# Sparse attention in pairs of batches: score rows in thirteen full tiles, values held in TensorE, probabilities divided on GpSimd

## The reference

```python
qkv = x @ qkv_w.T + qkv_b
q, k, v = (qkv[0], qkv[1], qkv[2])
true_scores = einsum('bhnd,bhmd->bhnm', q, k) * scale
pred_scores = einsum('bhnd,bhmd->bhnm', ex_quant(q), ex_quant(k))   # sign and power of two only
_, idx = top_k(pred_scores, 32)
topk_attn = softmax(take_along_axis(true_scores, idx))
attn = zeros.at[idx].set(topk_attn)
out = einsum('bhnm,bhmd->bhnd', attn, v) @ proj_w.T + proj_b
```

## Time and profile before

| | us |
|---|---|
| median of 3 runs | 1248.48 |
| lowest and highest | 1245.09, 1254.43 |
| the profiled execution, its own time | 1248.79 |
| its span in the profile | 1247.0 |
| first `take8` starts | 56.43 |
| last `finish` of the stage starts | 525.47 |

### The profile page before, as it was taken

The page is one execution under the profiler, slowest core; times in us unless marked ns, Lnnn a source line. Parts: engine busy times, 40 slices in busy tenths (PEclk is TensorE's granted clock), DMA queues, the critical chain, the costliest instruction groups (busy, mean ns, idle before and its releaser), DMA issues.

```text
span 1247.0 us, 24432 instructions
## 1 busy us (share of the span) xinstructions
PE 881.7 (71%) x6616; PEld 750.0 (60%) x6616; DVE 753.1 (60%) x4773; ACT 329.2 (26%) x1042; POOL 529.8 (42%) x745
## 2 busy tenths in 40 slices
PE   4788988898989898667400099987778656757830
PEld 4788878888888787444200088987556333633630
DVE  1399999999999999444553444334445344424533
ACT  0234433333433343144200033211111222213410
POOL 3244444444544443245376500043443544454235
PEclk9778888787878655555555599987775676878975
DMA  5123332323233330086021555444785544447833
GB/s 189 33 69 110 141 110 89 109 89 109 90 109 111 113 113 25 19 208 162 7 79 67 169 196 188 149 126 126 256 318 205 182 146 151 140 154 229 272 127 95
DMA packets 81318, 167.70 MB, mean 134 GB/s; under 512 B 12944, under 2 KB 39376, under 8 KB 79536
## 3 DMA queue, kind: packets, MB, share of 16 engines
q1 hardware_dynamic: 55824, 111.18, 27.5%
q10 hardware_dynamic: 14112, 32.12, 7.4%
q0 software_dynamic: 11264, 23.09, 6.3%
HBM read 84.81 MB, written 81.53 MB: 133 GB/s over the span
## 4 chain that ended last, share of the span: by engine, by line
PE 36%; DVE 32%; issue 18%; POOL 5%; DMA 4%; another core or an unknown queue 2%; ACT 2%; DVEq 1%; SPq 0%; POOLq 0%; ACTq 0%
DVE work L1301 13%; DVE top L1295 9%; PE bank L1166 6%; PE bank L1163 5%; PE bank L1212 5%; PE bank L1152 4%; PE bank L1210 3%; POOL early L700 2%; PE bank L1201 2%; PE bank L1099 1%; PE bank L925 1%; PE bank L984 1%; PE bank L1006 1%; POOL slots_g L707 1%
## 5 line engine op out<-in xcount | busy, mean ns | idle before, releaser
L1301 DVE MATCH_REPLACE8 work<-top,work 102x68 f32<-102x68 f32 x1024 | 204.7, 212 | 0.0
L1534 DVE COPY place<-bank 96x256 f32<-96x256 f32 x196 | 74.5, 416 | 149.2 <-PE bank L1152 98.3
L1295 DVE MAX8 top<-work 102x8 f32<-102x68 f32 x1024 | 145.5, 213 | 3.2 <-ACT tru L767 1.9
L1152 PE MATMUL bank<-ident,early 128*96 128x128 f32 x392 | 73.4, 316 | 102.9 <-DMA early<-slots_x 101.2
L886 ACT ACTIVATE m_y<-bank 128x128 f32<-128x128 f32 x196 | 52.5, 278 | 304.2 <-PE bank L1166 207.9
L1542 DVE COPY place<-bank 128x128 f32<-128x128 f32 x196 | 47.5, 286 | 133.0 <-PE bank L1201 73.1
L707 POOL DMA_INDIRECT slots_g<-early,s_all x68 | 66.1, 973 | 138.8 <-DVE early L1562 123.2
L1152 PEld LDWEIGHTS bank<-ident,early 128*96 128x96 f32 x392 | 52.3, 175 | 118.3 <-issue 117.9
L700 POOL DMA_INDIRECT early<-slots_h,s_all x68 | 65.2, 959 | 122.9 <-DMA slots_h<-m_y 102.5
L925 PE MATMUL bank<-xa,early 128*96 128x144 f32 x512 | 102.0, 352 | 16.8 <-DVE early L1319 16.0
L903 ACT ACTIVATE m_y<-bank 128x192 f32<-128x192 f32 x196 | 61.1, 331 | 170.5 <-PE bank L1212 78.8
(11 more groups left out here) (179 smaller groups left out, 1815.9 us busy)
## 6 DMA issues: line engine op xcount, KB each, us to landing
early<-slots_x SPq DMA_DIRECT2D x49, 384.0 KB
slots_y<-m_y ACTq DMA_DIRECT2D x49, 384.0 KB
slots_h<-m_y ACTq DMA_DIRECT2D x49, 256.0 KB
early<-slots_g SPq DMA_DIRECT2D x49, 256.0 KB
f_all<-in_f_know SPq DMA_DIRECT2D x16, 768.0 KB, 5.6
...
```

Of the source, the lines that this page charges most:

```text
L1152: last = nc.tensor.transpose(turn_bank[t][0:HALF, c * P:(c + 1) * P], m_x[:, d, t, c:D:2], ident[:])
L1295: last = nc.vector.max(top8[:, c, :], work[:, par, c, :])
L1301: last = nc.vector.match_replace(work[:, par, c, :], top8[:, c, :], work[:, par, c, :], TAKEN)
L1534: nc.vector.tensor_copy(m_halves[0:HALF, t], turn_bank[t][0:HALF, 0:2 * P].rearrange("p (c h s) -> p c h s", c=2, h=2)).then_inc(sem["m_xt ...
```

## The change

The stage goes by pairs of batches: slots are numbered q, 16 pairs instead of 32 batches, and the loop covers slots 2 to 11, two at a time. Most operations take both batches of the pair in one instruction.

- A pair has four sides (2 batches x 2 groups of six heads) of 408 score rows each. Each side gives 3 tiles of 128 rows, and the four remainders, padded from 24 to 32 rows, share one: 13 tiles of 128 rows for a pair, where two batches had 16 tiles of 102.
- The predicted scores and then the true ones use the same two PSUM banks (7 and 6 tiles), so the scores of a pair come in four steps, each with its own copy on ScalarE.
- The values are the operand held in PE (32 columns for a head, the other head's 16 being zeros; two heads add into one block of 32 rows), and the turned probabilities pass through. The result comes out already turned, so `turn_out` and its copy are gone.
- The sum of a row is taken by DVE over the probabilities (`total`), its reciprocal is `share`, and GpSimd multiplies the probabilities by it (`shared`) before PE turns them. `srec` and `o` are gone.
- The depth is less: in slot q, PE turns and uses the probabilities of pair q - 1, the same pair whose `share` is made in this slot, and `finish` is for pair q - 2, as the first item of DVE's slot.

```diff
-ROWS = HH * S // 4
+PAIRS = BATCH // 2
+SIDES = 4
+SIDE_ROWS = HH * S
+FULL = SIDE_ROWS // 128
+REST = 32
+SIDE = FULL * 128 + REST
+TILES = SIDES * FULL + 1
+SPLIT = 512 // S
...
-FIRST, LAST = 4, 24
+FIRST, LAST = 2, 12
...
-        work = sb("work", [ROWS, 2, 8, S])
-        tru = sb("tru", [ROWS, 2, 8, S])
-        top8 = sb("top8", [ROWS, 8, 8])
-        sc1 = sb("sc1", [ROWS, 2, 8, S])
-        sc2 = sb("sc2", [ROWS, 8, S])
-        smax = sb("smax", [ROWS, 8])
-        srec = sb("srec", [S, HEADS])
-        pT = sb("pT", [S, 2, HH * S])
-        oT = sb("oT", [HALF, 2, S])
-        h1b = sb("h1b", [S, 2, D])
+        hb = sb("hb", [S, 2, 2, D])
+        hbr = sb("hbr", [S, 2, 2, D])
+        hbp = sb("hbp", [S, 2, 2, D])
+        stat = sb("stat", [S, 2, 8])
+        mv = sb("mv", [S, 2, 8])
+        xn = sb("xn", [S, 2, D])
+        xnT = sb("xnT", [HALF, 2, 2, 2, S])
+        qk = sb("qk", [HALF, 2, 4, 2, S])
+        ek = sb("ek", [HALF, 2, 2, S], BF16)
+        qbd = sb("qbd", [HALF, SIDES, SIDE])
+        eqbd = sb("eqbd", [HALF, SIDES, SIDE], BF16)
+        v = sb("v", [S, 2, 2, HEADS, 2 * HD])
+        work = sb("work", [P, 2, TILES, S])
+        tru = sb("tru", [P, 2, TILES, S])
+        top8 = sb("top8", [P, TILES, 8])
+        sc1 = sb("sc1", [P, 2, TILES, S])
+        sc2 = sb("sc2", [P, TILES, S])
+        smax = sb("smax", [P, TILES])
+        total = sb("total", [P, TILES])
+        share = sb("share", [P, TILES])
+        pT = sb("pT", [S, SIDES, SIDE])
...
+        ps_score = bank[0:2]
+        ps_v, ps_proj, ps_k, ps_q, ps_pt, ps_eo = bank[2:8]
...
+            def slot(q, m):
+                back = runs(q, 1, PAIRS)
+                if back:
+
+                    pool.wait_ge(sem["gap_done"], q)
+                    if runs(q, 3, PAIRS):
+                        pool.wait_ge(sem["pt_mm"], (q - 2) * SIDES)
+                    nc.gpsimd.tensor_tensor(sc1[:, 1 - m], work[:, 1 - m], tru[:, 1 - m], ALU.add).then_inc(sem["masked"], 1)
+                if runs(q, 0, PAIRS - 2):
+                    spread(q + 1, 1 - m)
+                if back:
+                    pool.wait_ge(sem["smax_done"], q)
+                    if runs(q, 2, PAIRS):
+                        pool.wait_ge(sem["exp_done"], q - 1)
+                    nc.gpsimd.tensor_tensor(sc2[:], sc1[:, 1 - m], smax[:].unsqueeze(2).to_broadcast([P, TILES, S]),
                                             ALU.subtract).then_inc(sem["shifted"], 1)
+                if is_static(q) and q == 0:
+                    embed_rstd(2)
+                    embed_affine(2)
+                if back:
+                    residual(q - 1, 1 - m)
+                    pool.wait_ge(sem["share_done"], q)
+                    nc.gpsimd.tensor_tensor(sc1[:, 1 - m], sc1[:, 1 - m], share[:].unsqueeze(2).to_broadcast([P, TILES, S]),
+                                            ALU.mult).then_inc(sem["shared"], 1)
+                if runs(q, 0, PAIRS - 3):
+                    rstd(q + 2)
+                if runs(q, 0, PAIRS - 4):
+                    embed_rstd(q + 3)
+                    embed_affine(q + 3)
...
+            def copy_pt(q, i):
+
+                act.wait_ge(sem["pt_mm"], q * SIDES + (i + 1))
+                if i == 0 and runs(q, 1, PAIRS):
+                    act.wait_ge(sem["o_mm"], q * 2)
+                if i == 0:
+                    nc.scalar.activation(pT[:, :, FULL * P:SIDE], ps_pt[0:S, FULL * P:FULL * P + SIDES * REST].rearrange("p (i r) -> p i r", i=SIDES), ACT.Copy)
+                nc.scalar.activation(pT[:, i, 0:FULL * P], ps_pt[0:S, 0:FULL * P], ACT.Copy).then_inc(sem["pt_copied"], 1)
+
+            def copy_o(q, j):
+
+                act.wait_ge(sem["o_mm"], q * 2 + (j + 1))
+                if runs(q, 1, PAIRS):
+                    act.wait_ge(sem["proj_mm"], q * 2 + (j - 1))
+                nc.scalar.activation(oT[:, j], ps_o, ACT.Copy).then_inc(sem["ot_copied"], 1)
+
+            def slot(q, m):
+                front = runs(q, 0, PAIRS - 2)
+                back = runs(q, 1, PAIRS)
                 if front:
+                    copy_xt(q + 1, 1 - m)
+                if back:
+
+                    act.wait_ge(sem["topk"], q * 16)
+                    nc.scalar.activation(work[:, 1 - m], work[:, 1 - m], ACT.Identity, bias=gap_col[:], scale=-GAP).then_inc(sem["gap_done"], 1)
                 if front:
+                    copy_qk(q + 1, 1 - m)
+                if is_static(q) and q == 0:
+                    embed_bias(1)
+                    embed_copy(2)
+                if back:
+                    act.wait_ge(sem["shifted"], q)
+                    nc.scalar.activation(sc1[:, 1 - m], sc2[:], ACT.Exp, scale=SCALE).then_inc(sem["exp_done"], 1)
+                if m == 1 and runs(q, 0, PAIRS - 5):
+                    embed_bias(quad(q, m, 2))
+                if back:
+                    copy_pt(q - 1, 0)
+                if runs(q, 0, PAIRS - 4):
+                    embed_copy(q + 3)
                 if front:
+                    copy_scores(q + 1, 1 - m, work, 0, 0)
+                    copy_scores(q + 1, 1 - m, work, 1, 1)
+                if back:
+                    copy_pt(q - 1, 1)
+                if front:
+                    copy_scores(q + 1, 1 - m, tru, 0, 2)
+                if back:
+                    copy_pt(q - 1, 2)
+                    copy_o(q - 1, 0)
+                if front:
+                    copy_scores(q + 1, 1 - m, tru, 1, 3)
+                if back:
+                    copy_pt(q - 1, 3)
+                    copy_o(q - 1, 1)
+                if runs(q, 0, PAIRS - 3):
+                    scale(q + 2, m)
...
+            def turn_probs(q, par, i):
+
+                if i == 0:
+                    pe.wait_ge(sem["shared"], q + 1)
+                if i > 0 or runs(q, 1, PAIRS):
+                    pe.wait_ge(sem["pt_copied"], q * SIDES + i)
+                for c in range(FULL):
+                    last = nc.tensor.transpose(ps_pt[0:S, c * P:(c + 1) * P], sc1[:, par, i * FULL + c, :], ident[:])
+                if i == 0:
+                    last = nc.tensor.transpose(ps_pt[0:S, FULL * P:(FULL + 1) * P], sc1[:, par, TILES - 1, :], ident[:])
                 last.then_inc(sem["pt_mm"], 1)
 
+            def attend(q, par, j):
+
+                pe.wait_ge(sem["pt_copied"], q * SIDES + (2 * j + 2))
+                pe.wait_ge(sem["v_done"], q * 2 + (j + 1))
+                if j == 1 or runs(q, 1, PAIRS):
+                    pe.wait_ge(sem["ot_copied"], q * 2 + j)
                 for g in range(2):
+                    for second in range(2):
+                        for t in range(HH // 2):
+                            h = 2 * t + second
+                            last = nc.tensor.matmul(ps_o[2 * HD * t:2 * HD * (t + 1), g, :], v[:, par, j, HH * g + h, :],
+                                                    pT[:, 2 * j + g, h * S:(h + 1) * S], start=(second == 0), stop=(second == 1))
                 last.then_inc(sem["o_mm"], 1)
 
+            def project_out(q, j):
+                pe.wait_ge(sem["ot_copied"], q * 2 + (j + 1))
+                if j == 0 and runs(q, 1, PAIRS):
+                    pe.wait_ge(sem["h1_done"], q)
                 for g in range(2):
+                    last = nc.tensor.matmul(ps_proj[0:S, j * D:(j + 1) * D], oT[:, j, g, :], wp[:, g, :], start=(g == 0), stop=(g == 1))
                 last.then_inc(sem["proj_mm"], 1)
...
+            def slot(q, m):
+                front = runs(q, 0, PAIRS - 2)
+                back = runs(q, 1, PAIRS)
                 if front:
+                    turn_norm(q + 1)
+                    queries_keys(q + 1, 1 - m)
+                if is_static(q) and q == 0:
+                    embed_turn(2, 1, 0, 2)
+                if runs(q, 0, PAIRS - 1):
+                    values(q, m)
+                if runs(q, 0, PAIRS - 5):
+                    embed(quad(q, m, 2), 2 * m)
+                    embed(quad(q, m, 2), 2 * m + 1)
+                if back:
+                    turn_probs(q - 1, 1 - m, 0)
+                if runs(q, 0, PAIRS - 4):
+                    embed_turn(q + 3, quad(q, m, 1 + m), 1 - m, q + 2)
                 if front:
+                    scores(q + 1, 1 - m, eqbd, 0, 0)
+                    scores(q + 1, 1 - m, eqbd, 1, 1)
+                if back:
+                    turn_probs(q - 1, 1 - m, 1)
                 if front:
+                    scores(q + 1, 1 - m, qbd, 0, 2)
+                if back:
+                    turn_probs(q - 1, 1 - m, 2)
+                    attend(q - 1, 1 - m, 0)
+                if front:
+                    scores(q + 1, 1 - m, qbd, 1, 3)
+                if back:
+                    turn_probs(q - 1, 1 - m, 3)
+                    project_out(q - 1, 0)
+                    attend(q - 1, 1 - m, 1)
+                    project_out(q - 1, 1)
...
+            def slot(q, m):
+                take = runs(q, 0, PAIRS - 1)
+                back = runs(q, 1, PAIRS)
```

(31 more changed lines are left out.)

550 lines of the change are left out of this document (208 added, 342 removed).

## The result

The changed kernel takes **1304.8 us** (median of 4 runs, 1287.5 to 1312.9) where the kernel before took 1251.5 beside it on the same chip (1245.1 to 1263.8). The ratio is **1.034, 95% interval 1.026 to 1.043**: slower, by some 43 us. The ratio is taken over fast executions alone and leaves out the two slow ones of the changed kernel (1307.8, which is the profiled one, and 1312.9), so it lies under the ratio of the two medians, 1.043. The forecast was 1305 us against 1248.5.

The account below looks back on a forecast made before the run. It took a ring through PE, its length set by PE's clock, to bound the kernel. Pairs 1 to 10 22 us later, 11 to 14 30, the end 5: 1248.8 + 57 = 1306, forecast 1305 us, range 1238 to 1350.

Parts of the forecast that it names:

- the ring: Attention slot's path from projection through `share`, `shared` and PE's chain to the next projection: 25.9 us upper clock, 36.2 lower.
- The clock decides: In attention slots, the ring costs a bit over 1 us at PE's upper clock; the lower takes all savings and 7.4 more.
- To `share`, 13.2 (15.0): Ring's first part, from a projection's end until `share` is made: 13.2 us at PE's upper clock, 15.0 at the lower.
- PE behind `shared`, 11.0 (19.5): PE's chain after `shared`, from turns through projection and predicted scores: 11.0 us at the upper clock, 19.5 at the lower.
- rival 3: Products with the values overlap threefold by writing different rows: 49 us less than the forecast, 1256 us; chance 0.13.
- The alternation: Pairs 1 to 10 alternate low and high clock chains, 33.4 and 28.5 us, mean 31.0; 22 us later in all.
- Pairs 11 to 14: Late attention pairs, taken to have no embedding and a low clock: 36.2 us each, 30 us later in all.
- the sum: Whole attention stage: 22, 30 and 5 us later, 57 in all, added to the profiled 1248.8 us.
- Slot 0: First slot of the attention stage, without a pair behind it: 21.4 us.
- Rival 1: PE's clock stays up wherever there is embedding: pairs 1 to 10 at 26.8 us, 1263 us in all; chance 0.13.
- Rival 2: Chain behind `shared` short enough everywhere, under 13.7 us, also without embedding: 35 us earlier, 1214 us; chance 0.13.
- Rival 4: PE at the lower clock all along: pairs 1 to 10 at 36.2 us, 52 us more, 1357 us; chance 0.11.

Follow-up runs that it names:

- the fastest version: Changed kernel with images fetched early from ScalarE's queue and useless PE matmuls ahead of the wait for `shared` (12 in embedding slots, 41 in others): ratio 0.960.
- shortening the ring: Changed kernel with GpSimd subtracting ahead of its four spreads and DVE making `share` ahead of quantising: ratio 1.000 to the kernel before.
- the images' move: Changed kernel with only the images' loads moved from SyncE's queue to ScalarE's: ratio 1.046 to the kernel before.
- fillers: Useless PE matmuls ahead of the wait for `shared`, added to the changed kernel: 8 in embedding slots and 20 in others gave 1.003; 12 and 41 with the images' move, 0.960.
- the kernel with `norm` later: Changed kernel with the norm of the third pair's embedding moved later in DVE's slot 0, ahead of the third item: ratio 1.038.

## Why the prediction was right, and where its steps were off

**The bound moves to a ring: shown.** DVE idles for the projection; taking that wait to another place changes nothing (1.036), shortening the ring gives 40 us. DVE's own work was forecast at 24.7 us a slot; in the fastest version it is busy for 278 of 300 us in slots of 25.0, so 23.1.

**The clock decides: shown.** On one chip the changed kernel with the images' move gives 1.046, and the same with fillers 0.960. It is the same algorithm with more work on PE.

**To `share`, 13.2 (15.0): right for the lower clock, and not reached at the upper in the changed kernel.** From the projection's end to the turns behind `shared` it took 16.3 us without embedding (`finish` at 431.4, turns at 447.69), where 16.7 was forecast. Where the chain had been at the upper clock, it took 16.5 (`finish` at 210.5, turns at 226.96), not 14.9: between 209.5 and 211.4 PE waits 0.38 us for the projection's operand and 0.56 for the normalised rows, and its clock fell there (0.63 in the us from 211, then 0.50), so that queries and keys took the lower level's 3.9 us (forecast 3.8), not 2.1. In the fastest version, where fillers held the clock, it took 14.2 to 14.8 us in ten of thirteen slots, near the 14.9. Four of its terms (1.3, 1.2, 1.0 and 0.2) stand in the prediction without a row; in the changed kernel the exponential takes 0.94 us and the reciprocal 0.23.

**PE behind `shared`, 11.0 (19.5): mis-sized.** It took 9.6 at the upper clock, 15.2 at the lower. This is the term that rival 3 was about, and rival 3's mechanism is true: a pair's products take 2.1 us at the lower clock, not 5.7. That is 3.6 of the 4.3; the remaining 0.7 was not taken apart.

**The alternation did not come.** I had pairs 1 to 10 at 33.4 and 28.5 in turn. They took 31.1 to 32.0 and one 25.9; the ten last 306.6 us, 30.7 each, forecast 31.0. The step that failed is that the embedding would end at about 16 when `shared` comes at 16.7: it ended 1.96 to 3.36 us ahead of `shared` in nine of ten slots, and each time the chain behind that wait ran low. The forecast had the embedding bring the clock up; in the trace the clock is up when it begins, or within 0.5 us, so that it ended 14.3 us behind `finish` (242.0 to 256.3), not 16. A cheaper chain and a worse clock came to the same mean.

**Pairs 11 to 14 are not all without embedding.** Slot 11 still has it, as slots 22 and 23 had in the kernel before (PE embeds from 406.3 to 413.4 us and then waits 2.61 for `shared`). This cost the sum nothing that shows: slot 11 took 31.8 us, the next three 31.7, 31.4 and 31.4. What was off for all four is the chain, 36.2 forecast.

**Slot 0: missed.** 33.4 us in place of 21.4. I had counted DVE's work in it and not a wait of 10.0 us for the third pair's embedding; by the kernel with `norm` later, other waits for the same pair stand behind that one.

**The sum, again.** Pair 1 starts 13.2 us later than forecast (slot 0, and 1.2 of the start); pairs 1 to 10 take 3.4 less; pairs 11 to 14 take 126.2 in place of 144.8, 18.6 less; the last pair and the drain 42.0 in place of 48, 6 less. 57 + 13.2 - 3.4 - 18.6 - 6.0 = 42.2, and the last `finish` stands 567.9 - 525.5 = 42.4 later. So the forecast of 57 was 15 too much for the stage, and the median of 1304.8 meets 1305 only because the comparison's medians are 53 apart; by the ratio the forecast was some 14 us too high. It was right in sign, in the mechanism (ring and clock) and within its range. That it met the size to 1 us is luck: slot 0 is 13 too short, the rest 28 too long, and the medians' scatter made up what was left.

**The rivals.** Rival 1 (the clock stays up with embedding) was false as the kernel stood, and became true with fillers. Rival 2's condition was a chain under 13.7 us everywhere: it is 15.2 at the lower clock, so it failed by 1.5 us, and the fillers met it. Rival 3's price, 49 us off the forecast, did not come, although its mechanism did: slots 12 to 14 came 4.5 to 4.8 us under the 36.2 each, 3.6 of it by the cheaper products, but with embedding nearly every chain was low, where the forecast had every second one. Rival 4 (the lower clock all along) holds for nine chains in ten with embedding, but the embedding ahead of the chain ran at the upper level each time.

By the Trainium skill, "TensorE: Matmul & The Clock Gate", section "HAM oscillation — how this bites in real kernels", every chain would be low; the trace agrees, save for the one at 200.89 us, ahead of which PE waited 1.06 us.
